# Expert tiles that eleven routed batches fill run in the drain of the batch pipeline, and rows are added to the output by DMA

## The chip, the cores and the metric

One NeuronCore of a Trainium2 chip. The metric is the device time of one launch in microseconds (us). The core's engines run side by side and each takes its own instructions in order: PE (TensorE, matmuls), DVE (VectorE), ACT (ScalarE), POOL (GpSimd), SP (SyncE, which here only issues DMAs). They meet at semaphores alone. POOLq, ACTq and SPq in rows are the sequencers of those engines.

## What is computed

A transformer block with adaptive layer norm (16 batches of 256 tokens, width 128, 16 heads of width 8), followed by a mixture of 8 experts with the 2 best per token:

```python
mod = (_silu(c) @ wmod).reshape(B, 6, 1, -1)          # sa ca ga sb cb gb; |ga|, |gb| at least 0.25
h = _layernorm(x) * (1 + ca) + sa
x = x + ga * attention(h)                             # causal, rotary
h = _layernorm(x) * (1 + cb) + sb
xn = rmsnorm(h) * ln_w
vals, idx = top_k(xn @ Wg + bg, 2); topk_w = softmax(vals)
ffn = sum over the 2 chosen experts e of
      topk_w[e] * ((silu(xn @ W1a[e] + b1a[e]) * (xn @ W1b[e] + b1b[e])) @ W2[e] + b2[e])   # hidden width 512
x = x + gb * ffn
```

## The kernel before

**The pipeline over batches** (`pipeline`, L300) runs iterations i = -3 to 19. In iteration i each engine works on several batches at once, each in another stage: normalise (i+3), projections (i+2), scores by query for the maxima (i+1), probabilities and values (i, i-1), residual and second norm ("routing", batch i-2: `gate_out` L817, the residual add on POOL L492, statistics, `rstd` L506, `xhat` L767, `h_s` L512, `h_m` L514, `square` L637, `rms` L524), logits, top 2 and rank within the expert ("placing", batch i-3: `route` L833, `place` L858), and the sending of rows ("sending", batch i-4: `place_rows` L865 on DVE, `send_rows` L475 on POOL). An iteration is twelve steps k = 0 to 11 on PE, ACT and DVE; the order of the work within a step is written out by hand. On POOL the order of an iteration is the order of the lines L484 to L527. From i = 16 no new batch enters; iterations 16 to 19 are the drain: routing ends with i = 17, placing with 18, sending with 19.

**Routing by DMA.** Each expert has a region of DRAM rows (`expert_rows`), filled from its start. `send_rows` scatters 128 token rows in one indirect DMA of POOL, four times per batch (2 token blocks by 2 chosen experts); a row holds 128 words (the normed token as fp16 high and low part), a token number and the weight, 528 B in all. `filled` on DVE holds how many rows each expert has.

**The table.** After the pipeline DVE computes in 18 dependent steps (L970 to L1012) which expert and which first row each of NT = 39 tiles of 256 rows has. SP and ACT write a dummy tile behind the last row of each expert (`pad_experts`, L335), and SP waits for these and for all sends before it loads the first tile.

**The tile loop**, tile j on each engine:
- SP `load` (L433): waits until tile j-4 has been turned and named, reads the first row from the table and loads 256 rows to `g_in` (4 buffers).
- PE: `hidden` (L1304) computes for four blocks f of the hidden width 6 matmuls of 256 columns each, three for W1a and three for W1b (high x high, high x low, low x high); after f = 1 `turn_rows` (L1290) transposes the rows of tile j+1; then `project_out` (L1325) of tile j-1 with 24 matmuls into one of two banks.
- ACT (L703): silu of each block (L710), `xt` of the next tile (L684), the high part `hh` (L690), and `weigh` (L692) of tile j-2: two scalings by the token's weight into `y_sb` (L699).
- DVE (L1020): h32 = (b + bias) * silu (L1029), the low part `hl` (L1016), and the output bias (L1044) of tile j-2.
- POOL `scatter` (L556): copies number and weight of tile j+2, waits for the weighing of tile j, and writes its rows with two indirect DMAs (L563) to `expert_outs`, one row per token and chosen expert. No scatter waits for the one before it; a buffer `y_sb` is free again after four tiles.

**The finish** (SP L451, POOL L572, DVE L1057, ACT L731): for each batch SP loads its rows of `expert_outs` back, POOL adds the two experts' rows, DVE multiplies by gb (L1060) and adds the residual (L1064), ACT's queue stores the result.

Of the kernel before, what the change touches and what calls it, by code (L numbers as in the profile page):

```python
# [33 lines left out]
P = 128  # L34
# [4 lines left out]
HG = 4  # L39
# [3 lines left out]
NT = (B * S * K + E * (TS - 1)) // TS  # L43
REGION = B * S + TS
ROWS = E * REGION + TS
ROWW = D + 4
W_IDX, W_WGT = D, D + 1
NOUT = B * S * K
# [19 lines left out]
C_COS, C_SIN, C_E, C_BASE, C_TOK, C_POW, C_J = 0, 8, 24, 32, 40, 44, 48  # L68
# [34 lines left out]
def build(nc, x_in, wq, wk, wv, wo, ln_w, wg, bg, w1a, b1a, w1b, b1b, w2, b2, c_in, wmod, const32,  # L103
          const16, constb, dummy_in, out):
    ctx = ExitStack()
    with ctx:
# [11 lines left out]
        outs = nc.dram_tensor("expert_outs", [NOUT, D], F32).ap()  # L118
# [83 lines left out]
        tab = sb("tab", [P, 8, E])  # L202
        tab_i = sb("tab_i", [P, 2, E], I32)
        cmp_j = sb("cmp_j", [P, NT + 1, E])
# [11 lines left out]
        early = probs[:].rearrange("p j t -> p (j t)")  # L216
        silu_a = early[:, 0:FB * TS].rearrange("p (f t) -> p f t", t=TS)
        h32 = early[:, FB * TS:2 * FB * TS].rearrange("p (f t) -> p f t", t=TS)
        y_sb = early[:, 2 * FB * TS:2 * FB * TS + 4 * NS * D].rearrange("p (r s d) -> p r s d", s=NS, d=D)


        gb_sb = v_aug[:, 0:2].rearrange("p r c j g w -> p (r c j g w)").rearrange("p (b d) -> p b d", d=D)
        free = we_lo[:].rearrange("p n f -> p (n f)").bitcast(F32)

        def last(start, blocks):
            return free[:, start * NS * D:(start + blocks) * NS * D]

        y_in = last(0, 8).rearrange("p (r s k d) -> p r s k d", s=NS, k=K, d=D)
        ysum = last(8, 4).rearrange("p (r s d) -> p r s d", s=NS, d=D)
        ygate = last(12, 4).rearrange("p (r s d) -> p r s d", s=NS, d=D)  # L230
        res = last(16, 4).rearrange("p (r s d) -> p r s d", s=NS, d=D)

# [3 lines left out]
        chain_a16, chain_b16 = chain_a[:].bitcast(F16), chain_b[:].bitcast(F16)  # L236
# [7 lines left out]
        mod_out, gb_in = sem("mod_out"), sem("gb_in")  # L244
# [38 lines left out]
        table = sem("table")  # L283
# [6 lines left out]
        pe_y, vec_y, act_y = sem("pe_y"), sem("vec_y"), sem("act_y")  # L290
        y_sent = [sem(f"y_sent{r}") for r in range(4)]
        y_back = [sem(f"y_back{r}") for r in range(4)]
        pool_sum, vec_gate, vec_res = sem("pool_sum"), sem("vec_gate"), sem("vec_res")
        out_done = [sem(f"out_done{r}") for r in range(4)]

        TABLE_STEPS = 18
# [15 lines left out]
        def experts_of(eng):  # L312
# [10 lines left out]
            def read_next(j):  # L323
                m, r, _ = j
                if r == 3:
# [4 lines left out]
            for n in range(2):  # L330
                eng.reg_mov(before[n], 0)
            eng.load(regs, tile_e[0:1, 0:4])
            return known, read_next

        def pad_experts(eng, first):  # L335

            ends = [eng.alloc_register(f"end{n}") for n in range(4)]
            eng.load(ends, tab_i[0:1, 0, first:first + 4])
            for end in ends:
                v = eng.snap(end, min_val=0, max_val=ROWS - TS)  # L340
                eng.dma_start(rows[bass.ds(v, TS), :].rearrange("(s p) w -> p s w", p=P), dummy_sb[:]).then_inc(padded, 16)
# [14 lines left out]
        x_view = x_in.rearrange("b (s p) d -> p (b s) d", p=P)  # L356
        w1a_v = w1a.rearrange("e d (h f) -> e h d f", h=NS)
# [7 lines left out]
        def _(sp):  # L365
# [19 lines left out]
            def iteration(i, sending, placing, routing, closing, s2, s1, s0, norm):  # L385
# [22 lines left out]
                if s1:  # L408
                    place_max(i + 1, 1)

# [12 lines left out]
            sp.wait_ge(probs_used, B * 2 * HG)  # L423
            sp.dma_start(gb_sb, mod_rows[:, 3 * D:].unsqueeze(0).broadcast_to([P, B, D])).then_inc(gb_in, 16)
            sp.wait_ge(table, 1)
            pad_experts(sp, 0)
# [4 lines left out]
            sp.wait_ge(table, TABLE_STEPS)  # L431

            def load(j):  # L433
                r = j[1]

                if due(times(plus(j, -4), 1, 1)):
                    sp.wait_ge(pe_x, times(plus(j, -4), 1, 1))
                    sp.nop(nofuse=True)
                    sp.wait_ge(named.sem, named.after(plus(j, -4), "weight"))
                    sp.nop(nofuse=True)  # L440
                v = sp.value_load(tile_row[0:1, bass.ds(times(j, 1), 1)], min_val=0, max_val=ROWS - TS)
                sp.dma_start(g_in[:, r, :, :], rows[bass.ds(v, TS), :].rearrange("(s p) w -> p s w", p=P)).then_inc(g_arrived[r], 16)

            in_fours(sp, 0, NT, load)

# [3 lines left out]
            back = outs.rearrange("(b s p k) d -> b p s k d", s=NS, p=P, k=K)  # L449

            def finish(n):  # L451
                m, r, _ = n
                if due(times(plus(n, -4), 1, 1)):
                    sp.wait_ge(pool_sum, times(plus(n, -4), 1, 1))
                sp.dma_start(y_in[:, r], back[times(n, 1)]).then_inc(y_back[r], 16)

            in_fours(sp, 0, B, finish)
            for r in range(4):
                sp.wait_ge(out_done[r], 16 * (B // 4))
# [942 lines left out]
```

## Time and profile before

| | us |
|---|---|
| median of 3 runs | 564.38 |
| lowest, highest | 563.98, 567.52 |
| the profiled execution: its own time | 564.96 |
| its span, first to last instruction | 563.1 |

The span is 1.9 us shorter than the profiled execution's own time. Busy shares of the span: PE 80%, DVE 78%, ACT 66%, POOL 58%. An average over the whole says little here, since the program has four stages with different limits. Times in rows are from the span's start.

### The profile page before, as it was taken

What the parts mean: (1) busy time and instruction counts of PE and PEld (TensorE: products, weight loads), DVE (VectorE), ACT (ScalarE), POOL (GpSimd) and SP (SyncE); (2) the same over time, 40 slices, a digit from 0 to 9 for tenths busy, and PEclk for the clock granted to TensorE, in tenths of its full rate; (3) what the DMA queues carried; (4) which work ended last, traced back from release to release, by engine and by line L of the source; (5) the groups of instructions that cost most, each with busy time, mean ns of one, the idle gap of its engine ahead of it and who ended that gap; (6) DMA issues with size and microseconds to landing.
All of it is one profiled execution on the core that took longest, in us unless ns stands there. A gap on an engine that the chain in (4) does not pass through costs nothing.

```text
span 563.1 us, 20014 instructions
## 1 busy us (share of the span) xinstructions
PE 451.6 (80%) x6425; PEld 327.0 (58%) x6426; DVE 438.5 (78%) x1378; ACT 369.4 (66%) x916; POOL 325.0 (58%) x469
## 2 busy tenths in 40 slices
PE   4689999998988988889889313999999999999300
PEld 2445556665555655555555212988888888888300
DVE  4478888999999999999984661777777777777366
ACT  2347777877768777776864221988889888898300
POOL 3433355677777777877766772145455554545553
PEclk9999999999899999998995555999999999999855
DMA  7311111122102222022111323122222112121086
GB/s 216 122 30 46 33 34 39 55 69 63 61 16 69 69 64 59 18 67 70 36 42 40 99 77 102 31 59 66 53 57 59 48 53 57 50 57 36 15 266 181
DMA packets 46920, 37.74 MB, mean 67 GB/s; under 512 B 9234, under 2 KB 41573, under 8 KB 46848
## 3 DMA queue, kind: packets, MB, share of 16 engines
q1 hardware_dynamic: 36288, 25.05, 16.3%
q0 software_dynamic: 4544, 8.54, 4.7%
q10 hardware_dynamic: 6016, 3.21, 1.9%
q8 instruction: 43, 0.70, 0.5%
q14 instruction: 29, 0.24, 0.1%
HBM read 24.77 MB, written 12.78 MB: 67 GB/s over the span
## 4 chain that ended last, share of the span: by engine, by line
PE 35%; DVE 34%; issue 10%; ACT 8%; DMA 4%; SPq 4%; POOL 2%; DVEq 1%; ACTq 1%; POOLq 0%
DVE nmax L799 8%; PE bank L1315 4%; PE bank L1316 4%; PE bank L1317 4%; PE bank L1127 3%; DVE xhat L767 3%; PE bank L1336 3%; DVE probs L1029 3%; ACT qk_t L670 2%; PE bank L1169 2%; PE bank L1337 2%; PE bank L1134 2%; DVE hl L1016 2%; PE bank L1147 2%; PE bank L1338 2%
## 5 line engine op out<-in xcount | busy, mean ns | idle before, releaser
L563 POOL DMA_INDIRECT expert_outs<-probs,number_of x78 | 78.6, 1007 | 95.1 <-ACT probs L699 80.3
L799 DVE TENSOR_REDUCE nmax<-bank 128x2 f16<-128x384 f32 (+1 forms) x192 | 114.8, 600 | 20.6 <-PE bank L1134 18.5
L611 ACT ACTIVATE probs<-bank 128x512 f32<-128x512 f32 (+1 forms) x192 | 100.6, 524 | 45.6 <-PE bank L1159 44.6
L1029 DVE SCALAR_TENSOR_TENSOR probs<-bank,b_sb,probs 128x256 f32<-128x256 f32 x156 | 71.7, 479 | 53.0 <-ACT probs L710 52.3
L1127 PE MATMUL bank<-qk_t 24*64 24x64 f16 (+3 forms) x1024 | 74.5, 246 | 28.5 <-DVE nmax L799 19.4
L1315 PE MATMUL bank<-xt,we_hi 128*128 128x256 f16 x312 | 86.2, 276 | 2.8 <-DVE probs L1029 1.2
L1316 PE MATMUL bank<-xt,we_hi 128*128 128x256 f16 x312 | 86.0, 276 | 0.0
L1317 PE MATMUL bank<-xt,we_lo 128*128 128x256 f16 x312 | 85.9, 275 | 0.0
L480 POOL DMA_INDIRECT expert_rows<-send,pos_i x64 | 64.7, 1010 | 26.0 <-DVE tok L884 14.3
L690 ACT ACTIVATE hh<-probs 128x256 f16<-128x256 f32 x156 | 64.2, 411 | 20.3 <-DVE probs L1029 18.2
L1147 PE MATMUL bank<-qk_t 32*64 32x256 f16 (+3 forms) x1024 | 72.5, 240 | 1.7 <-DMA qk_t<-nmax_t 1.6
L1127 PEld LDWEIGHTS bank<-qk_t 24*64 24x64 f16 x1024 | 33.0, 107 | 68.5 <-DVE nmax L799 35.3
L710 ACT ACTIVATE probs<-bank,b_sb 128x256 f32<-128x256 f32 x156 | 68.3, 462 | 4.0 <-PE bank L1317 3.0
L1336 PE MATMUL bank<-we_hi,hh 128*128 x312 | 57.1, 222 | 4.7 <-DVE hl L1016 4.3
L1016 DVE TENSOR_TENSOR hl<-probs,hh 128x256 f16<-128x256 f32 x156 | 58.5, 416 | 0.0
L1338 PE MATMUL bank<-we_hi,hl 128*128 x312 | 55.3, 221 | 0.0
L1337 PE MATMUL bank<-we_lo,hh 128*128 x312 | 55.3, 221 | 0.0
L1169 PE MATMUL bank<-probs,v_aug 128*32 128x256 f32 (+3 forms) x1024 | 52.0, 324 | 0.0
L1134 PE MATMUL bank<-cb,c 128*128 128x128 bf16 (+1 forms) x192 | 48.9, 255 | 0.0
L1159 PE MATMUL bank<-cb,c 128*128 128x128 bf16 (+1 forms) x192 | 46.7, 243 | 0.0
L1147 PEld LDWEIGHTS bank<-qk_t 32*64 32x64 f16 x1024 | 35.9, 106 | 4.7 <-DMA qk_t<-nmax_t 2.2
L1336 PEld LDWEIGHTS bank<-we_hi,hh 128*128 128x128 f16 x312 | 30.8, 99 | 12.5 <-issue 11.6
(157 smaller groups left out, 1087.3 us busy)
## 6 DMA issues: line engine op xcount, KB each, us to landing
g_in<-expert_rows SPq DMA_DIRECT2D x39, 132.0 KB
qk_t<-nmax_t SPq DMA_DIRECT2D x256, 0.5 KB
mod_b<-mod_rows SPq DMA_DIRECT2D x16, 256.0 KB
we_lo<-expert_outs SPq DMA_DIRECT2D x16, 256.0 KB, 3.8
wstage<-in_L_ffn_W1a_dram SPq DMA_DIRECT2D x16, 128.0 KB
wstage<-in_L_ffn_W1b_dram SPq DMA_DIRECT2D x16, 128.0 KB
wstage<-in_L_ffn_W_dram SPq DMA_DIRECT2D x16, 128.0 KB
out_dram<-we_lo ACTq DMA_DIRECT2D x16, 128.0 KB, 3.4
```

Source lines behind the costliest of these rows:

```text
L563: pool.indirect_dma_start(out=outs, out_offset=bass.IndirectOffsetOnAxis(ap=number_of[:, r, s:s + 1], axis=0), in_=y_sb[:, r, s, :], in_of ...
L611: nc.scalar.activation(probs[:, k // 3, first:end], col_bank[k % 2][:, 0:end - first], ACT.Exp, scale=SM_SCALE).then_inc(probs_ready, 1)
L710: nc.scalar.activation(silu_a[:, f], banks[f][:, 0:TS], ACT.Silu, bias=b1_sb[:, 0, bass.ds(e * FB + f, 1)]).then_inc(act_silu, 1)
L799: nc.vector.tensor_reduce(nmax[:, pair, js[0]:js[-1] + 1, 3 * DK + c], scores, AX.X, ALU.max, negate=True).then_inc(max_ready, 1)
L1016: nc.vector.tensor_tensor(hl[:, j[1] % 2, f], h32[:, f], hh[:, j[1] % 2, f], ALU.subtract).then_inc(vec_hl, 1)
L1029: nc.vector.scalar_tensor_tensor(out=h32[:, f], in0=banks[f][:, TS:2 * TS], scalar=b1_sb[:, 1, bass.ds(e * FB + f, 1)], in1=silu_a[:, f], ...
L1127: mm(row_bank[u % 2][ROW * n:ROW * n + ROW, seg * m:seg * m + seg], qk_t[rows_g, b % 3, j, ROW * c:ROW * c + ROW], qk_t[rows_g, b % 3, HG ...
L1147: mm(col_bank[k % 2][ROW * n:ROW * n + ROW, at:at + S - ROW * c], qk_t[group, b % 3, HG + j0 + jn, ROW * c:ROW * c + ROW], qk_t[group, b % ...
L1315: mm(o, we_hi[:, n, at], x_hi, start=(n == 0), stop=False, skip_group_check=True)
L1316: mm(o, we_hi[:, n, at], x_lo, start=False, stop=False, skip_group_check=True)
L1317: t = mm(o, we_lo[:, n, at], x_hi, start=False, stop=True, skip_group_check=True)
L1336: mm(o, hh[:, par, f, tok_s], we_hi[:, 2, at], start=(s == 0 and f == 0), stop=False, skip_group_check=True)
```

## The change

- **Two tables.** When 11 batches have been placed, DVE copies the counts (`count_early`), and in iteration 15 it computes a first table (`first_tiles`) of the EARLY = 15 tiles that these rows are sure to fill. The second table (`last_tiles`), for tiles 15 to 38, is computed in iteration 19, spread over its steps.
- **Tiles in the drain.** In each step k of iterations 16 to 19 PE, ACT and DVE first do one block f of one tile (`tile_step`), so 3 tiles per iteration and tiles 0 to 11 in the drain. SP loads tiles 0 to 3 at the end of iteration 15 and three per drain iteration. POOL does tile 0's scatter in iteration 16, three in each of 17, 18 and 19 (the one of tile `drained - 2` ahead of everything else in the iteration, two later). Tiles 12 to 14 follow, then 15 to 38 in the loop.
- **The output is added up in DRAM.** x after attention is stored to `out` per batch (SP, iteration i for batch i-2). Each scatter adds its rows to `out` by an indirect DMA with an add (`compute_op=ALU.add`). A token's two rows may lie in neighbouring tiles, so each scatter waits until the scatter before it has landed (`y_sent`). `expert_outs` and the finish are gone.
- **The gate rides in the row.** gb of the batch is put into the row to send (`gates`, one DMA of SP per batch), so a row is 260 words (1040 B) instead of 132, and a tile's load 260 KB instead of 132 KB. `weigh` is moved from ACT to DVE: y times weight times gate, two instructions. Therefore `load(j)` also waits for the weighing of tile j-4.
- One PSUM bank instead of two for the turned rows (`chain_b`) and for y (`o_bank`), since the drain uses the others. In the drain the exponential of the routing is a power on POOL, so that ACT keeps its table for silu. All eight pads are issued by SP.

```diff
+EARLY_B = 11
+EARLY = -(-(EARLY_B * S * K - E * (TS - 1)) // TS)
-ROWW = D + 4
+ROWW = 2 * D + 4
@@ sync, end of iteration(i)
+                if routing:
+                    sp.wait_ge(pool3a.sem, pool3a.after(i - 2, "resid"))
+                    sp.dma_start(out_view[:, NS * (i - 2):NS * (i - 1), :], x_sb[:, NS * (i - 2):NS * (i - 1), :]).then_inc(x_out[i - 2 >= EARLY_B], 16)
+                if placing:
+                    gates(i - 3)
+                if i == B - 1:
+                    sp.wait_ge(early_table.sem, len(early_table.names))
...
+                    for n in range(4):
+                        load(tile_number(n))
+                if i >= B:
+                    n = 3 * (i - B) + 3
+                    for n in range(max(n, 4), n + 3):
+                        load(tile_number(n))
@@ load(j)
+                    sp.wait_ge(vec_w, times(plus(j, -4), NS, NS))
+                    sp.nop(nofuse=True)
@@ sync, after the pipeline
+            sp.wait_ge(last_table.sem, last_table.after(0, "ends"))
+            pad_experts()
...
+            sp.wait_ge(last_table.sem, len(last_table.names))
+            in_fours(sp, EARLY, NT, load)
-            in_fours(sp, 0, B, finish)
@@ gpsimd, iteration(i)
+                drained = 3 * (i - B)
+                if i == B:
+                    pool.wait_ge(x_out[0], 16 * EARLY_B)
+                    name_rows(tile_number(0))
+                    name_rows(tile_number(1))
+                if i > B:
+                    scatter(tile_number(drained - 2))
...
+                if i > B and not i == B + 3:
+                    scatter(tile_number(drained - 1))
...
+                if placing and i >= B:
+                    nc.gpsimd.tensor_tensor(egap[:], c32[:, C_EXP:C_EXP + NS], gap[:], ALU.pow).then_inc(gap_exp, 1)
+                if B <= i < B + 3:
+                    scatter(tile_number(drained))
...
+                if i == B + 3:
+                    scatter(tile_number(drained - 1))
+                    scatter(tile_number(drained))
@@ scatter(j)
-                pool.wait_ge(act_y, times(j, NS, NS))
+                pool.wait_ge(vec_w, times(j, NS, NS))
+                before = plus(j, -1)
+                if due(times(before, 1, 1)):
+                    pool.wait_ge(y_sent[before[1]], times((before[0], 0, 1), 32, 32))
                 pool.nop(nofuse=True)
                 for s in range(NS):
-                    pool.indirect_dma_start(out=outs, ..., bounds_check=NOUT - 1, oob_is_err=False).then_inc(y_sent[r], 16)
+                    pool.indirect_dma_start(out=out_rows, ..., bounds_check=NOUT - 1, oob_is_err=False, compute_op=ALU.add).then_inc(y_sent[r], 16)
@@ scalar
-                    if f == 2 and finished:
-                        weigh(plus(j, -2))
@@ vector
+                if i == B - 2:
+                    count_early()
...
                 for k in range(NK):
+                    if i >= B:
+                        tile_step(*tile_of(i, k))
...
+                    if i == B - 1 and k == 3:
+                        first_tiles()
+                    if i == B + 3:
+                        last_tiles(k)
@@ vector, tile_step(j, f)
+                if f == 0 and finished:
+                    bias_out(plus(j, -2), before_last)
+                vec.wait_ge(act_silu, times(j, FB, f + 1))
...
+                if f == 0 and finished:
+                    weigh(plus(j, -2))
+            def weigh(j):
+                r = j[1]
+                vec.wait_ge(vec_y, times(j, 1, 1))
+                vec.wait_ge(named.sem, named.after(j, "weight"))
+                if due(times((j[0], 0, 1), 32)):
+                    vec.wait_ge(y_sent[r], times((j[0], 0, 1), 32))
+                vec.nop(nofuse=True)
+                for s in range(NS):
+                    nc.vector.scalar_tensor_tensor(out=y_sb[:, r, s], in0=yb[:, r % 2, s], scalar=weight_of[:, r, s:s + 1],
+                                                   in1=g_in[:, r, s, W_GATE:], op0=ALU.mult, op1=ALU.mult).then_inc(vec_w, 1)
@@ tensor
                 for k in range(NK):
+                    if i >= B:
...
+                        tile_step(*tile_of(i, k))
```

## Rows read from the trace of the kernel before

**Rows 1.** The page: the span in 40 equal slices, in tenths
```profile
PE   4689999998988988889889313999999999999300
...
PEclk9999999999899999998995555999999999999855
```
**Rows 2.** Busy time by stage; columns as named in its second line
```profile
core 0: us, PE busy (x) PEld busy (x) DVE busy (x) ACT busy (x) POOL busy (x), PEclk, DMA share, GB/s
...
304.80:318.00 13.20, 9.04 (x58) 5.68 (x58) 7.68 (x39) 3.28 (x12) 8.38 (x12) 0.50 0.31 90
318.00:329.40 11.40, 2.94 (x14) 2.33 (x14) 6.02 (x34) 2.59 (x9) 8.36 (x10) 0.50 0.11 38
329.40:343.60 14.20, 0.28 (x5) 0.19 (x4) 7.53 (x39) 2.42 (x4) 8.39 (x9) 0.50 0.40 119
343.60:361.50 17.90, 14.79 (x143) 12.66 (x144) 8.32 (x22) 11.16 (x29) 0.96 (x7) 0.77 0.21 54
361.50:532.60 171.10, 160.97 (x1887) 139.87 (x1885) 126.22 (x330) 145.03 (x401) 88.82 (x149) 0.99 0.19 51
532.60:563.10 30.50, 0.00 (x0) 0.00 (x0) 19.07 (x32) 0.00 (x0) 13.85 (x17) 0.50 0.68 206
```
**Rows 3.** The scatter line L563: ns min/median/max, first and last start
```profile
L563 POOL DMA_INDIRECT expert_outs<-probs,number_of x78: 971/979/1130, 361.5 to 532.6; - x78
...
DMA to landing us min/median/max: 2.1/2.3/3.8
```
**Rows 4.** The chain that ended last, 529 to 542: start us, us, what
```profile
529.83 0.70 ACT probs L699 x2
...
531.34 0.97 POOL expert_outs L563
532.31 0.30 issue
532.62 2.11 DMA expert_outs<-probs,number_of
```
**Rows 5.** POOL in order of time, 515 to 563 (last scatter, finish)
```profile
531.34 0.97 POOL L563 DMA_INDIRECT expert_outs<-probs,number_of  x1 [0.86 <-ACT probs L699]
532.62 0.97 POOL L563 DMA_INDIRECT expert_outs<-probs,number_of  x1 [0.30 <-issue]
```
**Rows 6.** Transfers and table on the chain, 280 to 348
```profile
294.56 1.54 DMA qk_t<-nmax_t
...
343.67 2.22 DMA g_in<-expert_rows
```
**Rows 7.** POOL in order of time, 298 to 346 (one drain iteration)
```profile
306.80 0.73 POOL L492 TENSOR_TENSOR x_sb<-x_sb,gated 128x256 f32<-128x256 f32 x1 [1.97 <-DVE gated L821]
308.44 0.99 POOL L480 DMA_INDIRECT expert_rows<-send,pos_i  x1 [0.92 <-DVE tok L884]
309.46 0.68 POOL L499 TENSOR_TENSOR send<-xn,send 128x256 f16<-128x256 f32 x1
...
314.69 0.72 POOL L524 TENSOR_TENSOR rms<-ms,c 128x2 f32<-128x2 f32 x1 [0.42 <-DVE rank L860]
```
**Rows 8.** POOL in order of time, 440 to 450 (naming of a tile)
```profile
446.42 0.21 POOL L553 COPY number_of<-g_in 128x2 int32<-128x2 int32 x1
446.54 0.20 POOL L554 COPY weight_of<-g_in 128x2 f32<-128x2 f32 x1
```
**Rows 9.** Groups of DVE: the tile loop's, and the nearest to weighing
```profile
L1029 DVE SCALAR_TENSOR_TENSOR probs<-bank,b_sb,probs 128x256 f32<-128x256 f32 x145 | 66.5, 479 | 38.8 <-ACT probs L710 38.1 <-issue 0.5
L1016 DVE TENSOR_TENSOR hl<-probs,hh 128x256 f16<-128x256 f32 x147 | 55.1, 416 | 0.0
...
L831 DVE SCALAR_TENSOR_TENSOR xn<-h_m,rms,lnw_sb 128x128 f32<-128x128 f32 x8 | 2.4, 342 | 1.1 <-POOL rms L524 1.1
```
**Rows 10.** PE alone in stretches of 2 us: us, PE busy (x), granted clock, DMA
```profile
348.00:350.00 2.00, 2.00 (x12) 0.50 0.32 78
350.00:352.00 2.00, 2.00 (x14) 0.52 0.21 58
352.00:354.00 2.00, 2.00 (x22) 1.00 0.27 68
```
**Rows 11.** DVE in order of time, 280 to 346 (first and last table step)
```profile
333.51 0.17 DVE L972 CAST tab_i<-filled 128x8 int32<-128x8 f32 x1
...
338.39 0.18 DVE L1011 CAST tile_e<-tj 128x40 int32<-128x40 f32 x1
```

More of the change, by code:

```diff
@@ L117, in build @@
         rows = nc.dram_tensor("expert_rows", [ROWS, ROWW], F32).ap()
-        outs = nc.dram_tensor("expert_outs", [NOUT, D], F32).ap()
         c32 = sb("c32", [P, NC32])
@@ L282, in build @@
         sent = [sem("sent0"), sem("sent1")]
-        table = sem("table")
+        early_table = steps("early_table", "clear count count_i tiles_i tiles weight sum cmp e part offset row0 row row_i expert expert_i left done")
+        last_table = steps("last_table", "ends count count_i tiles_i tiles left sum next net weight cmp e part offset row0 row row_i expert expert_i")
         padded = sem("padded")
@@ L328, in read_next, with read_first, is_tile, tile_of @@
                     eng.load(regs, tile_e[0:1, bass.ds(4 * (m + 1), 4)])
[L330 to L341, printed above, removed]
+            def read_first():
+                eng.wait_ge(early_table.sem, len(early_table.names))
+                for n in range(2):
+                    eng.reg_mov(before[n], 0)
+                eng.load(regs, tile_e[0:1, 0:4])
+            return known, read_next, read_first
+        def is_tile(j, n):
+            return isinstance(j[0], int) and j == tile_number(n)
+        def tile_of(i, k):
+            step = NK * (i - B) + k
+            return tile_number(step // FB), step % FB
         def in_fours(eng, first, end, body):
@@ L690, in high @@
                 nc.scalar.activation(hh[:, j[1] % 2, f], h32[:, f], ACT.Copy).then_inc(act_hh, 1)
-            def weigh(j):
-                r = j[1]
-                if due(times((j[0], 0, 1), 32)):
-                    act.wait_ge(y_sent[r], times((j[0], 0, 1), 32))
-                act.wait_ge(vec_y, times(j, 1, 1))
-                act.wait_ge(named.sem, named.after(j, "weight"))
-                for s in range(NS):
-                    nc.scalar.activation(y_sb[:, r, s], yb[:, r % 2, s], ACT.Copy, scale=weight_of[:, r, s:s + 1]).then_inc(act_y, 1)
@@ L739, in _, with tile @@
+            def tile(j, more=True):
+                for f in range(FB):
+                    tile_step(j, f, more)
+            pipeline(iteration)
+            for n in range(3 * FB, EARLY):
+                tile(tile_number(n))
+            in_fours(act, EARLY, NT - 1, tile)
+            tile(tile_number(NT - 1), more=False)
         @block.vector
@@ L1010, in _, with count_early @@
-            vec.wait_ge(table, 17)
-            nc.vector.tensor_copy(tile_e[:], tj[:, 0]).then_inc(table, 1)
-            vec.wait_ge(table, TABLE_STEPS)
+            base, iota = c32[:, C_BASE:C_BASE + E], c32[:, C_J:C_J + NT + 1]
+            each, padded_each = slice(1, E + 1), slice(0, E + 1)
+            count, tiles, zero, ends, done, left, weight, net = (tab[:, n] for n in range(8))
+            def count_early():
+                nc.vector.memset(tab[:], 0.0).then_inc(early_table.sem, 1)
+                vec.wait_ge(early_table.sem, early_table.after(0, "clear"))
+                vec.wait_ge(vec_place.sem, vec_place.after(EARLY_B - 1, "filled"))
+                nc.vector.tensor_tensor(count[:, each], filled[:], base, ALU.subtract).then_inc(early_table.sem, 1)
@@ L1325, in project_out, with tile @@
+                t.then_inc(pe_ab, 1)
+                if f == 1 and more:
+                    turn_rows(plus(j, 1))
+                if f == FB - 1:
+                    if due(times(j, 1)):
+                        project_out(plus(j, -1), last)
+                    read_next_experts(j)
+            def tile(j, more=True):
+                e = known_experts(j)[0]
+                for f in range(FB):
+                    tile_step(j, f, more)
+                return e
             def project_out(j, e):
@@ L1339, in project_out @@
                 t.then_inc(pe_y, 1)
-            def tile_and_last(j, more=True):
-                e, last = hidden(j, more)
-                project_out(plus(j, -1), last)
-                return e
-            turn_rows(tile_number(0))
-            hidden(tile_number(0))
-            in_fours(pe, 1, NT - 1, tile_and_last)
-            project_out(tile_number(NT - 1), tile_and_last(tile_number(NT - 1), False))
+            pipeline(iteration)
+            for n in range(3 * FB, EARLY):
+                tile(tile_number(n))
+            in_fours(pe, EARLY, NT - 1, tile)
+            project_out(tile_number(NT - 1), tile(tile_number(NT - 1), False))
 def constants():
```

405 lines of the change are left out of this document (218 added, 187 removed).

## The prediction

> **What bounds the kernel now.** I read the page's slices first [rows 1]: PE is dense in two blocks, with a hole between them in which the granted clock is at its lower level, and empty at the end. The busy time by stage puts numbers on it [rows 2]. From 304.8 (the last probabilities of batch 15 are just done) to 343.6 (the first load of a tile) lies the drain with the table and the pads: 38.8 us in which PE is busy for 9.04 + 2.94 + 0.28 = 12.3 us, and that at clock 0.50, so it is some 6.1 us of work at full clock. From 343.6 to 532.6 runs the tile loop with PE busy nearly throughout. From 532.6 to 563.1 PE has nothing: the last scatter lands and the finish reads, adds and stores.
>
> The tile loop's rate is read from its scatters [rows 3]: 78 issues start from 361.5 to 532.6, the second of a tile 1.28 after the first [rows 5], so 38 tiles take 171.1 - 1.28 = 169.8 us, 4.47 us each.
>
> The new thing is the wait of each scatter for the landing of the one before, so the length of one scatter matters. The chain at the end shows it unhidden [rows 4]: the weighing ends at 530.53, POOL's first indirect DMA starts at 531.34 (0.81 to wake), takes 0.97, 0.30 of issue, and the second transfer's 2.11 begin at 532.62. The list of POOL [rows 5] has the second issue start at that same 532.62: the landing counts from the start of the issue, not from its end. So a plain scatter needs 0.81 + 0.97 + 0.30 + 2.11 = 4.19 us from release to landing; with the median landing of 2.3 [rows 3] it is 4.38. That is 0.1 under the tile's 4.47, before anything is paid for the add.
>
> **The change part by part.**
>
> *The add.* No row of before shows an indirect DMA that adds. It has to read the old row from DRAM as well. From below: nothing, if that read runs beside the read of the new one. A gain is excluded, since it does all that the plain write does. From above: a whole second landing, 2.3. Nearest are two transfers [rows 6]: SBUF to SBUF lands in 1.54, DRAM to SBUF in 2.22; a DRAM read in the way costs 0.7 (sizes differ, so this is rough). I take 0.7: a scatter in a chain of scatters takes P = 4.38 + 0.7 = 5.1 us, bounds 4.4 and 6.7. The issue itself (0.97) I leave as it is; if it grew by half, P would grow by 1.0, which is inside these bounds.
>
> *The loop when P is above the tile's time.* POOL then sets the rate; PE, ACT and DVE wait through the four `y_sb` buffers (`weigh(j)` waits for scatter j-4). The naming of the next tile (0.21 + 0.20 [rows 8]) lies in the landing, which outlasts the issue by 2.3 - 0.98 = 1.3.
>
> *The weighing moves to DVE.* Nearest is the 128x128 product at 0.342 us [rows 9]: two make 0.7. DVE's tile was four of 0.479, four of 0.416 and one output bias of about 0.42: 4.0 in sum of durations (neighbours overlap in the rows), of which 126.2/38.3 = 3.3 busy [rows 2]. With 0.7 it stays at 4.0 of 4.47: it fits, and ACT loses as much. Cost 0, at worst 0.2 a tile, hidden while P is 5.1; without this cover it is 27 x 0.2 = 5 us.
>
> *Larger load, later released.* `load(j)` now starts only after `weigh(j-4)`, in DVE's tile j-2, and PE turns its rows in tile j-1, about 4.5 us later. The load needs the register read and issue, about 0.9, and 2.22 for half the bytes [rows 6]; I put 2.7 on 260 KB: 3.6. It fits with 0.9 to spare. Behind the waiting SP stand only further loads. Were a load to land in 4.3 as the worst 256 KB ones may, PE would stall some tenths per tile; P covers that too.
>
> *One bank for y and one for the turned rows.* `project_out(j)` waits for the bias add of j-1, which DVE does while PE spends 24 of 48 matmuls on the hidden blocks of j+1; nothing is paid. The same for the turned rows: their copy ends a half tile before.
>
> *The drain.* Iterations 16 to 19 now hold 12 tiles. Three sizes of it can be had. PE alone: 12 x 4.47 + 6.1 = 60 us. Nothing overlapped: 38.8 + 53.6 = 92 us. And POOL, which is in order and has the most to do. Its own work per full iteration is five elementwise operations of 0.7 and four sends of 0.99 with 0.3 each [rows 7], 8.4 busy [rows 2], 9.6 with gaps. A scatter adds 2 x 0.98 + 2 x 0.3 + 0.3 for the names, 2.85, and about 0.45 where it has to be woken: 3.3; the landing of the one before is covered by the work between, except for the last two. Iteration 16 took 13.2 for its waits; with one scatter, a second naming and the power (0.8) it is 17.4. Iteration 17: 9.6 + 0.8 + 3 x 3.3 = 20.3. Iteration 18, without the residual and norm, has four sends (5.1), 0.7, 0.8 and three scatters: 16.5. Iteration 19: four sends, one scatter, and two in a chain at P: 5.1 + 3.3 + 10.2 = 18.6. Sum 73 us. I take POOL's sum, since PE's 60 lies under it and the steps lock the engines together. At 304.8 PE is at the lower clock; it rose about 5 us after PE became dense at 347 [rows 10], so iteration 16 loses a few us on PE, which POOL's 17.4 covers.
>
> *Tables and pads.* 18 steps took from 333.5 to 338.6, 5.1 us [rows 11]. The first table is some 16 of them, narrower, about 3.5 us, in iteration 15, where DVE waits in places anyway; I count 1 us. The second lies in iteration 19 beside POOL's 18.6. Pads and the wait for the last sends then have tiles 12 to 14 (15 us) as cover; without these they cost the 3 to 4 us that they did.
>
> *Main part.* SP gets two DMAs more per iteration (gate, x), each some 0.5 us of its queue, behind the second `place_max`; what waits for SP next is a maximum of the next iteration, half of it later. Rows sent are twice as long. Counted as 0, at worst 0.5 x 16 = 8.
>
> *Removed.* The finish: from 532.62 + 2.11 = 534.7 to 563.1, 28.4 us.
>
> **The sum.** 304.8 + 1 (first table) + 73 (drain, scatters 0 to 9 landed) + 29 x 5.1 (scatters 10 to 38, the last landing included) = 304.8 + 1 + 73 + 147.9 = 526.7 span. The profiled execution's time is 1.9 above its span and the median 0.6 below that time: 528 us.
>
> **The rivals.**
>
> *A. The tile sets the rate.* If the add costs under 0.1 to 0.2, POOL follows PE again. For it: the plain scatter is 0.1 shorter than the tile. Against: an add without any cost. After the drain 27 tiles x 4.5 and the tail of the last one (before: last matmuls near 527.4 to landing at 534.7, with the last hidden part 8.3): 304.8 + 1 + 73 + 121.5 + 8.3 + 1.3 = 510 us.
>
> *B. The drain does not overlap.* POOL waits inside a scatter for `weigh`, DVE waits at `rstd` or `rms` for POOL, PE for DVE, so that latencies add. For it: in-order queues, and each of the old iterations is itself such a chain. Against: the scatters are placed behind the step that frees them. With 92: 304.8 + 1 + 92 + 147.9 + 1.3 = 547 us.
>
> *C. The other side: the add doubles the landing.* Place: POOL's wait for `y_sent` in each scatter. Price: 2.3 more, P = 6.7, and 304.8 + 1 + 73 + 29 x 6.7 + 1.3 = 574 us. It decides from P = (564.4 - 380.1)/29 = 6.4 on. For it: all 29 scatters of the last part stand in one chain, each 0.1 us is 2.9 us. Against: the rows are 512 B, eight per DMA engine and issue, so latency and not volume makes the landing. The Trainium skill speaks for this rival: "Collectives: The Full Stack" (The bandwidth ceiling) says that a reduction in the DMA engines needs two source reads on one ring and measured 1.93 times the time of a copy. By it the landing would be 4.4, P 6.5 and the kernel 568 us; no row of before shows an adding DMA.
>
> **How the numbers follow.** Forecast 0.55, A 0.23, B 0.12, C 0.10. A measurement tells about 1% from no change: faster is under 558.7, slower over 570. The forecast, A and nearly all of B are faster; C is slower, and a P near 6.2 falls in between: 0.83, 0.08, 0.09. The range reaches from under A, 507, to P = 6.0 or B with a somewhat dearer add, 556.
>
> **What would show it.** Right: after the drain POOL's line of the adding DMA has starts 5.1 apart per tile, and its idle time is ended by the landing of `out`, not by DVE; PE waits about 0.7 a tile for DVE; the landing is 3.0. The drain is 73 us with the clock at its upper level after the first few us. The span ends with a landing. The forecast is wrong if the period differs from 5.1 by over 0.3 (9 us), if POOL waits for the weighing (A), if the drain is over 85 (B), or if the landing is over 4.3 (C).

## The result and the profile after

The changed kernel takes 703.37 us, median of four runs (702.48 to 708.62), beside 564.92 (563.98 to 567.52) for the one before: ratio 1.246, 95% interval 1.239 to 1.254. Forecast were 528 us and a range of 507 to 556. The profiled execution has a span of 700.4 us, 173.7 over the forecast's sum of 526.7.

First the page after, the slices of [rows 1] (each is 17.5 us now).

```profile
span 700.4 us, 20061 instructions
...
PE   4889994955955846856755827766767977877820
...
PEclk9999997868778879768878657989987999999965
```

PE loses its density from slice 7 on, some 105 us in, in the middle of the old pipeline, in which I had changed nothing by my own count. The hole of before at slices 23 to 25 is gone, but nearly every slice behind the seventh is thinner, and the last two (2 and 0) are close to empty again, though there is no finish any more.

Where the time came from is read by stage. The borders are now the end of POOL's 48th send of rows (304.8 in [rows 2]), the landing of scatter 9, the end of PE's work but for its last 1.2 us, and the end. The landing is set at 519.9, the median 3.3 us behind the start of the issue; this one in fact landed at 522.9, so 3 us of the chain's part below belong to the drain's. The first line is of the kernel before, for the same work as the line below it.

```profile
core 0: us, PE busy (x) PEld busy (x) DVE busy (x) ACT busy (x) POOL busy (x), PEclk, DMA share, GB/s
60.00:304.80 244.80, 219.60 (x3822) 140.29 (x3818) 225.34 (x786) 178.07 (x416) 174.12 (x233) 0.97 0.18 51
...
60.00:415.70 355.70, 239.91 (x3852) 149.93 (x3850) 236.95 (x801) 178.46 (x417) 174.32 (x234) 0.80 0.22 58
415.70:519.90 104.20, 74.09 (x786) 63.51 (x787) 71.91 (x262) 57.59 (x146) 65.34 (x79) 0.86 0.43 99
519.90:673.00 153.10, 117.14 (x1311) 97.81 (x1310) 101.49 (x280) 91.44 (x225) 86.70 (x100) 0.95 0.40 67
673.00:700.40 27.40, 1.22 (x12) 0.95 (x9) 1.65 (x5) 0.00 (x0) 12.66 (x11) 0.50 0.12 9
```

| part | forecast | measured | off by |
|---|---|---|---|
| start to the end of the pipeline | 305.8 | 415.7 | +109.9 |
| drain, to the landing of scatter 9 | 73 | 104.2 | +31.2 |
| scatters 10 to 38 | 147.9 | 180.5 | +32.6 |
| finish | 0 | 0 | 0 |

ACT and POOL are busy as long as they were before: POOL has its 174 us of work, now in 355.7 us in place of 244.8. So this is waiting. The groups of waits name it (us in total, times, longest):

```profile
POOL expert_rows L498 <- DMA send<-mod_rows: 116.2, 12, 12.1
PEld bank L1211 <- DVE nmax L811: 115.1, 42, 9.9
...
DVE xhat L779 <- POOL rstd L531: 90.8, 12, 10.2
ACT qk_tok L700 <- POOL turned L566: 82.4, 12, 9.3
```

The first of these is the source and the others are its echo: POOL waits twelve times, some 10 us each, for the DMA that puts the gate into the rows to be sent; DVE and ACT wait for POOL, PE for DVE. One such iteration on the queue of SP and then on POOL (start, us, instruction, and in brackets the idle time before it):

```profile
342.21 4.38 SPq L459 DMA_DIRECT2D qk_t<-nmax_t  x8
346.65 0.40 SPq L411 DMA_DIRECT2D out_dram<-x_sb  x1
347.09 0.54 SPq L450 DMA_DIRECT2D send<-mod_rows  x1
```

```profile
330.58 0.98 POOL L498 DMA_INDIRECT expert_rows<-send,pos_i  x1 [9.37 <-DMA send<-mod_rows]
...
345.67 0.73 POOL L517 TENSOR_TENSOR x_sb<-x_sb,gated 128x256 f32<-128x256 f32 x1
...
356.56 0.99 POOL L498 DMA_INDIRECT expert_rows<-send,pos_i  x1 [10.16 <-DMA send<-mod_rows]
```

This is a ring. POOL is let into its first send at 330.58. Behind that send stand the power, the turning and the keys of the next batches; from these PE makes scores and DVE maxima, whose DMAs SP issues until 346.59. Only then comes the gate's DMA, at 347.09. It takes 8.5 us to land (its line's median), and POOL is let into the next first send at 356.56. That is 16.5 + 9.5 = 26.0 us, and an iteration is 26.9 long between two residual additions where it was 17.4 (typical distances).

The scatter line, for [rows 3] and [rows 5]:

```profile
L599 POOL DMA_INDIRECT out_dram<-qk_tok,number_of x78: 1538/1549/1958, 442.9 to 694.6; - x78
...
DMA to landing us min/median/max: 2.7/3.3/6.3
```

```profile
563.45 1.55 POOL L599 DMA_INDIRECT out_dram<-qk_tok,number_of  x1 [2.29 <-DMA out_dram<-qk_tok,number_of]
565.30 1.54 POOL L599 DMA_INDIRECT out_dram<-qk_tok,number_of  x1 [0.30 <-issue]
...
569.22 1.55 POOL L599 DMA_INDIRECT out_dram<-qk_tok,number_of  x1 [2.06 <-DMA out_dram<-qk_tok,number_of]
```

The period (from one tile's first issue to the next tile's) is 5.77 here. Issue went from 0.98 to 1.55, the landing from 2.3 to 3.3. By the forecast's own formula P = 0.81 + 1.55 + 0.30 + 3.3 = 5.96; the mean over tiles 15 to 38 is 5.88, where the forecast had 5.1 and the kernel before 4.40. Most of these waits stand in the trace under the name issue (79.5 us in 69 pieces, only 10.7 under the landing), as the profile saw no releaser. The times tell it: from tile 15 on a scatter starts 0.81 us after the landing of the one before in the median, wherever the trace has that landing, and its own weighing has then been over for 11 us or more. From 673 on PE has a last 1.2 us of work, and POOL goes on through its chain to the end, 27.4 us later.

Right behind the drain the chain is slower than that. SP writes the eight pads there, 260 KB each, and the DMA engines are busy all the time (share 1.00). The landings of the next scatters stretch (median 5.2 us from 508 to 530), and PE waits for a tile's load. The pads, the stretch of time, POOL's scatter 10 and PE:

```profile
L445 SPq DMA_DIRECT2D expert_rows<-dummy_sb x8: 372/397/925, 514.2 to 519.4; - x8
...
514.00:523.00 9.00, 5.89 (x68) 4.95 (x65) 7.11 (x21) 5.30 (x13) 3.47 (x4) 1.00 1.00 273
...
523.67 1.55 POOL L599 DMA_INDIRECT out_dram<-qk_tok,number_of  x1 [5.17 <-issue]
...
528.53 0.61 PE L1390 MATMUL bank<-c,g_in 128*128 128x128 f16 x4 [7.33 <-DMA g_in<-expert_rows]
```

### The profile page after: what moved, and what is told of

The parts are those of the page before. It is cut to its first block and busy times, and to the rows that moved or that the text cites. A ratio compares the mean times of both kernels' runs of the same rounds, so it can differ in the third digit from the quotient of the medians.

```text
span 700.4 us, 20061 instructions
## 1 busy us (share of the span) xinstructions
PE 476.9 (68%) x6425; PEld 338.2 (48%) x6426; DVE 449.3 (64%) x1443; ACT 353.6 (50%) x835; POOL 361.6 (52%) x456
## 3 DMA queue, kind: packets, MB, share of 16 engines
q1 hardware_dynamic: 43760, 33.06, 18.5%
## 5 line engine op out<-in xcount | busy, mean ns | idle before, releaser
L599 POOL DMA_INDIRECT out_dram<-qk_tok,number_of x78 | 123.4, 1582 | 91.5 <-issue 79.5
L1105 DVE SCALAR_TENSOR_TENSOR qk_tok<-bank,b_sb,silu_a 128x256 f32<-128x256 f32 x156 | 73.4, 480 | 48.7 <-ACT silu_a L731 46.5
L779 DVE TENSOR_SCALAR xhat<-x_sb,mv,rstd 128x128 f32<-128x128 f32 x64 | 35.7, 598 | 91.7 <-POOL rstd L531 90.8
L721 ACT ACTIVATE hh<-qk_tok 128x256 f16<-128x256 f32 x156 | 64.5, 413 | 38.9 <-DVE qk_tok L1105 36.6
L731 ACT ACTIVATE silu_a<-bank,b_sb 128x256 f32<-128x256 f32 x156 | 71.4, 468 | 21.3 <-PE bank L1408 20.5
L1253 PE MATMUL bank<-probs,v_aug 128*32 128x256 f32 (+3 forms) x1024 | 60.5, 365 | 0.0
L1092 DVE TENSOR_TENSOR hl<-qk_tok,hh 128x256 f16<-128x256 f32 x156 | 60.1, 427 | 0.0
L1390 PE MATMUL bank<-c,g_in 128*128 128x128 f16 x156 | 16.5, 232 | 57.7 <-DMA g_in<-expert_rows 57.6
L700 ACT ACTIVATE qk_tok<-turned 128x256 f16<-128x256 f32 x32 | 13.2, 411 | 82.6 <-POOL turned L566 82.4
L1218 PE MATMUL bank<-cb,c 128*128 128x128 bf16 (+1 forms) x192 | 50.3, 262 | 0.0
```

The lines of the kernel that those rows point to most:

```text
L599: pool.indirect_dma_start(out=out_rows, out_offset=bass.IndirectOffsetOnAxis(ap=number_of[:, r, s:s + 1], axis=0), in_=y_sb[:, r, s, :], i ...
L721: nc.scalar.activation(hh[:, j[1] % 2, f], h32[:, f], ACT.Copy).then_inc(act_hh, 1)
L731: nc.scalar.activation(silu_a[:, f], banks[f][:, 0:TS], ACT.Silu, bias=b1_sb[:, 0, bass.ds(e * FB + f, 1)]).then_inc(act_silu, 1)
L1105: nc.vector.scalar_tensor_tensor(out=h32[:, f], in0=banks[f][:, TS:2 * TS], scalar=b1_sb[:, 1, bass.ds(e * FB + f, 1)], in1=silu_a[:, f], ...
```

## The experiments

Each is the changed kernel with one edit unless said otherwise; before means a kernel before run on the same chip beside it.

**e1, the gate's place in SP's queue.**

```diff
+                if placing:
+                    gates(i - 3)
                 if s1:
                     place_max(i + 1, 0)
...
-                if placing:
-                    gates(i - 3)
```

> The changed kernel with SP's gate DMA moved ahead of the two groups of max transfers in its iteration; its waits and bytes are the same. Theory G (place in the queue): the changed kernel's batch pipeline is 111 us longer (POOL's last send of iteration 15 ends at 415.7 instead of 304.8), because POOL waits for a gate that SP issues only behind the last maxima and that lands 8.5 us later. Then POOL's 116 us of waiting for the gate go to under 10, the last send of iteration 15 ends at 305 to 320, and the time falls from 703 to 590 to 615. Rival T (traffic: rows twice as long, 16 more DMAs of 256 KB, the stores of x): the pipeline stays over 390 and the time over 680, wherever the gate DMA stands.

Measured: 587.53 us, 1.040 of before (1.026 to 1.055). The same windows:

```profile
60.00:305.80 245.80, 221.98 (x3853) 142.02 (x3846) 225.88 (x801) 178.63 (x417) 174.00 (x233) 0.96 0.35 86
305.80:406.30 100.50, 75.19 (x791) 62.40 (x790) 71.97 (x264) 58.16 (x148) 65.78 (x79) 0.90 0.42 95
406.30:584.10 177.80, 115.14 (x1315) 95.88 (x1312) 101.96 (x283) 90.89 (x224) 99.81 (x110) 0.91 0.35 59
```

The pipeline ends at 305.8, as forecast, with every DMA still issued and the same landing of 8.4: POOL's wait for the gate is gone from the list. So 116 us of the change's time are the place of one DMA in an in-order queue, 110 of them in the pipeline. The time is 2.5 us under the 590 to 615 expected. What is left, 584.1 against 526.7, is drain (+27.5) and chain (+29.9).

**e2, no gate at all.** `gates(i - 3)` and POOL's wait for it are out.

> The changed kernel without the gate DMAs and POOL's wait for them, so the expert part of the output is left out (it is multiplied by zero); every other instruction runs. Theory G: the same gain as with the gate issued first, 590 to 610, and the difference between the two, up to 10 us, is what the gate's 256 KB cost as traffic. Rival T: if the doubled rows and the stores are what slows the pipeline, it stays over 390 at POOL's last send of iteration 15 and the time over 680.

Measured: 581.46 us, 1.030 (1.016 to 1.043). Against e1 that is 6 us, with overlapping intervals, and 8.5 us under the 590 to 610 expected. The pipeline ends at 308.4, no earlier than in e1: in its new place the gate's DMA costs the pipeline nothing. The drain is the shorter part, 92.0 for 100.5 us.

**e11, old place, quicker DMA.** The gate's DMA stays where the change put it, but reads 512 different rows (of `x`) in place of 512 times one row, so the gates are other numbers. **e7** is the same on top of e1.

```diff
-mod_rows[b:b + 1, 3 * D:].unsqueeze(1).broadcast_to([P, K * NS, D])
+x_in.rearrange("(c b2) t d -> c (b2 t) d", b2=2)[b // 2].rearrange("(p n) d -> p n d", n=K * NS)
```

> The changed kernel with the gate DMA where it was, but reading 512 different rows (landing 3.3 instead of 8.4 us; other numbers are multiplied in). It parts the 111 us of the pipeline into place and landing. Theory: each of the 12 waiting iterations gets 5.1 us back, 61 in all: pipeline to 350 to 360, time 635 to 650. Rival (the wait is set by the place alone, behind the last maxima, or the landing alone): over 690, or under 600.

> The kernel with the gate issued first, its DMA reading 512 different DRAM rows of 512 B instead of one row 512 times (other numbers than the gate's are multiplied in). Theory H (the one row read over and over is what makes the landing 8.4 us): it falls to 3 to 4.5 us. Rival D (512 pieces of 512 B into a strided tile cost this anyway): it stays over 7. The time stays within 8 us of 587 by both, since nothing waits for this DMA there.

Measured: e11 626.87 us, 1.113 (1.105 to 1.121), 76 less than the changed kernel; e7 one run of 578.07. The gate's DMA in the changed kernel, in e7 and what waits for it in e11:

```profile
DMA to landing us min/median/max: 8.2/8.5/10.1
```

```profile
DMA to landing us min/median/max: 3.2/3.3/4.6
```

```profile
L450 SPq DMA_DIRECT2D send<-in_L_attn_x_dram x16: 545/594/1531, 108.4 to 406.7; - x16
...
  POOL expert_rows L498: 55.3, 12
```

The same bytes in as many pieces (43760 packets on that queue in both) to the same places land in 3.3 in place of 8.4: reading one DRAM row 512 times is what was slow. In e7 a partition's four rows are neighbours in DRAM; whether that plays a part was not run. And the ring passes it on one for one: 26.9 less 5.2 gives 21.7 per iteration, and e11 has 21.2 in the mean (19.2 to 22.6). Its pipeline ends at 352.0, within the 350 to 360 expected; in all it beat the expectation of 635 to 650, since the drain got some 11 us shorter too. Speed of the DMA alone does not cure the order, though: 12 waits of 4.6 remain. In e7 nothing waits for this DMA, and yet it is 9.5 us under e1, where within 8 was expected: one run, but its drain shows where, as e5 does next.

**e5, the gate fetched once and copied on the chip.** One 64 KB DMA per batch, then a copy by ACT into the rows.

```diff
-dma_start(mod_b[:, i % 2, :], mod_rows[i:i + 1, :].broadcast_to([P, 4 * D]))
+dma_start(mod_b[:, i % 2, :], mod_rows[i:i + 1, 0:3 * D].broadcast_to([P, 3 * D]))
+dma_start(gate_b[:, i % 4, :], mod_rows[i:i + 1, 3 * D:].broadcast_to([P, D]))
...
+activation(send[..., W_GATE:], gate_b[:, bs % 4, :].unsqueeze(1).broadcast_to([P, K * NS, D]), ACT.Copy)
```

> The changed kernel with the gate brought to SBUF once per batch (64 KB, 128 rows of 512 B, beside mod_b) and copied into the rows to send by one ACT instruction, instead of a DMA of 512 rows of 512 B. Theory G: the gate was dear only by its place and landing, so this is within 8 us of the kernel with the gate issued first (587): 580 to 592, and POOL waits for nothing of the gate. Rival: the copy of about 0.6 us on ACT delays the sends and costs 16 x 0.6 = 10 us or more: over 595.

Measured: 576.35 us, 1.024 (1.011 to 1.037), 11 under e1 and 4 under the 580 expected at least, though the intervals of the two overlap. The stages show where. Scatter period 5.88 in both; the drain is 92.0 in place of 100.5. In e1 scatters 2 and 5 (from 0) start 11.85 and 11.23 after the ones before them, here 8.02 and 6.43. PE's wait for loads of tiles is 44.6 us in e1 and 37.6 here. The slow read is what does it: e7 differs from e1 in nothing else and has 8.06 and 8.35 there, and a drain of 96.1. What exactly it holds up was not looked into.

**e3, chain without the add, and e4, add without the chain.** In e3 the scatter overwrites. In e4 every (token, expert) has its own row in `outs` and scatters don't wait for each other.

```diff
-bounds_check=NOUT - 1, oob_is_err=False, compute_op=ALU.add)
+bounds_check=NOUT - 1, oob_is_err=False)
```

```diff
-                before = plus(j, -1)
-                if due(times(before, 1, 1)):
-                    pool.wait_ge(y_sent[before[1]], times((before[0], 0, 1), 32, 32))
```

> The changed kernel with the scatter's add taken away (a plain write, so residual and first expert's row are lost from the output); each scatter still waits for the landing of the one before. Theory A (the add itself is dear): issue back from 1.55 to 0.98, landing from 3.3 to 2.3, a scatter from 5.9 to 4.4 apart; with 29 scatters behind the drain 703 falls by 40 to 50 to about 658. Rival W (the waiting is dear, not the add): scatters stay over 5.3 apart and the time falls by under 20.

> The changed kernel whose scatters add into rows of their own (one row per token and chosen expert in a separate tensor, so the two are not summed and the output lacks the expert part), and therefore need no wait for the scatter before. Theory A with the chain: the wait for the landing is gone, a scatter costs POOL 2 x 1.55 + 2 x 0.3 + 0.3 = 4.0 and a wake, 4.5 to 4.8 apart, and the 27 us tail in which PE has nothing shrinks to under 12; time 650 to 665. Rival (POOL's issue is the bound, not the landing): over 5.3 apart, time over 680.

Measured: e3 658.60 us, 1.166 (1.145 to 1.187), scatter period 4.81 (4.4 was expected); e4 659.49, 1.168 (1.149 to 1.186), period 4.71. Each is 44 to 45 us under the changed kernel. The add and the wait are not two prices that sum: take either away and the chain no longer sets the period alone. From tile 15 on 23 of 24 scatters of e4 start about 0.8 us after their own weighing, and in e3 16 of 24 start within 1.4 us of it. In the changed kernel none does. The line of e3 has the plain price back:

```profile
L599 POOL DMA_INDIRECT out_dram<-qk_tok,number_of x78: 967/978/1516, 439.5 to 646.3; - x78
...
DMA to landing us min/median/max: 2.1/2.8/6.0
```

**e12, the add alone, in the kernel before.** `compute_op=ALU.add` on its unchained scatters; 16 DMAs of SP set the rows to zero during the pipeline.

> The kernel before with the add in its scatters (onto rows that 16 further DMAs of SP have set to zero in the pipeline), no scatter waiting for another. Theory (the add alone is hidden; only in a chain is it paid): POOL's tile is 2 x 1.55 + 2 x 0.3 + 0.3 = 4.0 us, under the tile's 4.47, so the loop keeps its 4.47 and only the last landing and issues come late, 2 to 3 us; with the zeroing 565 to 572. Rival (POOL with a wake of 0.8 is over 4.47 per tile): 4.8 per tile, 578 or more.

Measured: 566.07 us, median of ten, 1.0031 (0.9991 to 1.0071). The scatter line and POOL's last issues:

```profile
L571 POOL DMA_INDIRECT expert_outs<-probs,number_of x78: 1543/1552/1845, 360.4 to 532.9; - x78
```

```profile
525.54 1.54 POOL L571 DMA_INDIRECT expert_outs<-probs,number_of  x1 [0.30 <-issue]
527.39 1.55 POOL L571 DMA_INDIRECT expert_outs<-probs,number_of  x1 [0.30 <-issue]
529.24 1.54 POOL L571 DMA_INDIRECT expert_outs<-probs,number_of  x1 [0.30 <-issue]
```

POOL pays 78 x 0.57 = 45 us more for its issues, and the kernel takes the same time: two issues are 3.7 us of a tile that lasts 4.43. An adding scatter is free off the path. In a chain it is 0.57 of issue and 1.0 of landing per tile by the formula; the period fell by 1.1 without it (5.88 to 4.81 in e3), since the weighing then comes about as late as the landing.

**e8, e1 with plain scatters, and e9, e10: the load split.** PE in e1 still waits 44.6 us for tile loads, and a load waits for `vec_w` on account of the gate in it. In e9 (on e1) and e10 (on e8) the x part is loaded without that wait, and the gate part by a DMA of its own:

```diff
-                    sp.wait_ge(vec_w, times(plus(j, -4), NS, NS))
...
-dma_start(g_in[:, r, :, :], rows[bass.ds(v, TS), :]...)
+dma_start(g_in[:, r, :, 0:W_GATE], rows[bass.ds(v, TS), 0:W_GATE]...)
+                if due(times(j, 1)):
+                    load_gate(plus(j, -1))
```

> The kernel with the gate issued first and the scatter's add replaced by a plain write, each still waiting for the one before (residual and first expert's row are lost). Theory A: the same 45 us as in the changed kernel, 587 to 537 to 548; scatter 9 lands 80 to 92 us after the pipeline instead of 100, then 29 scatters of 4.7 to 4.9. Rival (once the gate is out of the way another limit holds the loop): over 560.

> The kernel with the gate issued first and each tile's load in two DMAs: the 132 words with token, number and weight without the wait for the weighing of tile j-4, and the gate's 128 words with that wait, one tile later in SP's order. Theory C (the chain of adding scatters, 5.9 to 6.1 apart, is the bound and PE's 50 us of waiting for loads are only its echo): the loop stays at 6.0 per tile, only the drain may lose up to 10: 575 to 588. Rival L (the late load is a bound of its own): 560 or less.

> The same two DMAs per load in the kernel with the gate issued first and plain scatters in a chain. Here the scatters (4.4 of release to landing) leave room, and PE waited 68 us for loads against 8 us in the part with the short rows. Theory L (load released by the weighing is the next limit under the add): PE's wait for loads falls under 25 us and the time from 540 to 518 to 532. Rival (the plain chain of 4.4 plus what POOL waits for the weighing is the bound): 536 or more.

Measured: e8 543.69 us (two runs, 539.46 and 547.91; its rows are of the longer one), within its 537 to 548 and 44 under e1, so the add has about the same price with and without the ring; e9 591.21, 1.049 (1.041 to 1.058); e10 538.54, 0.956 (0.949 to 0.962). The expectation's 68 us of waiting for loads in e8 counts PE's 32.5 and the weight load's 35.2 for the same loads. PE's group of the turned rows (busy, mean ns, then idle before it) in e9 and in e10:

```profile
L1401 PE MATMUL bank<-c,g_in 128*128 128x128 f16 x156 | 16.8, 236 | 31.8 <-DMA g_in<-expert_rows 31.8
```

```profile
L1401 PE MATMUL bank<-c,g_in 128*128 128x128 f16 x156 | 15.5, 224 | 9.1 <-DMA g_in<-expert_rows 9.1
```

e9 missed its 575 to 588: PE waits 13 us less for loads, and the period is 5.97, as before the edit (5.88). A late load was the echo of a late POOL. In e10 the waits shrink from the 32.5 of e8, and the period stays too, 4.76 after 4.77; it missed its 518 to 532, and is within 1 us of the quicker run of e8. So the load is not what holds the plain chain at 4.8, either. By the formula a plain chain has P = 0.81 + 0.98 + 0.30 + 2.3 to 2.8 = 4.4 to 4.9, which would do it. e4, with no chain, has 4.71 because POOL waits for the weighing. Why the tile itself takes 0.3 longer there than before (two products more on DVE, longer loads, for which PE waits 6.4 us from 540 on) was not taken apart.

**e6, the early tiles alone.** Two tables and tiles in the drain stay. Rows are short again, scatters plain, without a chain and into own rows, gate and sum in the finish of before; the weighing stays on DVE, as a product with one scalar. This computes the whole output.

```diff
-ROWW = 2 * D + 4
+ROWW = D + 4
...
-scalar_tensor_tensor(out=y_sb[:, r, s], in0=yb[:, r % 2, s], scalar=weight_of[:, r, s:s + 1], in1=g_in[:, r, s, W_GATE:], ...)
+tensor_scalar(y_sb[:, r, s], yb[:, r % 2, s], weight_of[:, r, s:s + 1], None, ALU.mult)
...
-oob_is_err=False, compute_op=ALU.add)
+oob_is_err=False)
```

> One part of the change alone: two tables and tiles in the drain, with the row of 132 words, no gate in it, plain scatters without a chain into expert_outs and the finish of the kernel before. Theory (the tiles in the drain are worth what was forecast, add and gate ate it): pipeline to 306, drain 70 to 85 with 12 tiles in it, 27 tiles of 4.5 and the tail of 8, finish 28: 533 to 550 us, faster than before by 3 to 5%. Rival B (the drain does not overlap with the tiles even without the add, latencies add): drain over 92, time over 555, no gain left.

Measured: 543.52 us, median of five; 0.9665 of before (0.958 to 0.975), within the 533 to 550 expected. It beats both kernels. Its windows, from its quickest run (537.58): drain, tile loop, finish.

```profile
303.20:382.00 78.80, 66.18 (x704) 57.23 (x704) 63.37 (x242) 50.33 (x129) 52.34 (x77) 0.89 0.23 63
382.00:508.70 126.70, 113.85 (x1399) 102.46 (x1396) 104.89 (x303) 96.69 (x242) 67.01 (x112) 1.00 0.23 63
508.70:535.50 26.80, 0.00 (x0) 0.00 (x0) 18.85 (x32) 0.00 (x0) 13.35 (x16) 0.50 0.76 235
```

In [rows 2] the drain was 38.8 us with PE busy for 12.3; here PE is busy for 66.2 of 78.8. The period of tiles 15 to 38 is 4.18, under the 4.40 of before, with the weighing off ACT (the edit nearest to this; it wasn't run alone). The finish it keeps costs 26.8 us.

## Why the prediction was wrong, by its own steps

- *Main part* is the step that failed, with nearly two thirds of the miss (109.9 of 173.7 us). It listed the two new DMAs of SP and asked what waits behind them on SP ("what waits for SP next is a maximum of the next iteration"), priced that at 0, at worst 8 us, and never asked who waits for the DMAs themselves. POOL's first send does (`pool.wait_ge(gate_in...)` in `send_rows`), it stands ahead of everything from which SP's next maxima come, and the DMA comes after these maxima. The two orders close to a ring of 26 us around a pipeline step of 17.4. The wait was in the diff, and the ring could have been summed: nearly a whole step of 17.4 from the first send to the last maxima (16.5 it was), then a landing and a wake, so over 17.4 with any landing. e1 shows the place to be the cause; e11 shows that the length of the DMA goes into it one for one.
- *The same step* gave that DMA no landing at all. It is 8.5 us (3.3 with different source rows), and this excess is 5.2 x 12 = 62 of the 110. No row above showed such a read; the nearest in the trace of before is `v_aug<-mod_rows`, 1024 KB from 16 rows of 512 B, each read 128 times, which landed in 9.3.
- *The add*: the mechanism was right, the size off. I took 0.7, on the landing alone; measured are 1.0 on the landing and 0.57 on the issue, which I had left "as it is". P came out at 5.96 by the formula, inside my bounds of 4.4 and 6.7, and at 5.88 in the mean (5.4 to 6.5) between scatters. My "if it grew by half, P would grow by 1.0" counted both issues of a scatter; my formula has one of them, as the landing counts from the start of the second, so it is 0.5. 29 x 0.86 = 25 of the 32.6 us; most of the rest lies right behind the drain, where scatter 10 starts 8.95 after scatter 9 and the next five are 5.8 to 7.4 apart, beside the pads.
- *The drain*: 73 by POOL's sum. With plain, unchained scatters and short rows it is 78.8 (e6). My sum has two scatters in a chain at 5.1; at 3.3 each and with a last landing of 1.3 it is about 71, so the method falls some 8 us short. With the price of the add, 10 scatters x 2 x 0.57 = 11.4 more, the sum is 84; measured 92.0 with the copied gate (e5), 100.5 with the slow one (e1), 104.2 as changed, and 107.2 to the landing itself. It ended above the 85 at which I had said that it fails. What makes the last 8 us of e5 (chain, longer rows, the store of x) was not taken apart.
- *The weighing on DVE* at 0 was right where the chain covers it: it is done 11 us or more before its scatter. Without this cover the runs differ. In e4 POOL waits for it and the tile has 4.71; in e6, where it is a product with one scalar and the rows are short, the tile got shorter by 0.22. No run has the weighing alone on the other engine.
- *Larger load*: "it fits" was right in effect. It lands in 3.0 (2.7 forecast), and freeing it of its wait gained nothing (e9, e10).
- *One bank, names, tables*: nothing of them shows. The first table was counted as 1 us, and the pipeline of e1 ends 1.0 later than that of before, all of its other additions included; but e6, e7 and e2 end at 303.2, 304.2 and 308.4, so this is luck as much as measure.
- *The pads* were to have tiles 12 to 14 as cover. They do not hide: no tile load is issued from 513.3 to 525.5, PE waits 7.3 us for one, and the landings beside them stretch. In e4, where no chain covers it, scatter 13 starts 14.4 us after scatter 12.
- *Removed*: 28.4 us of finish are gone, as forecast; the tail of POOL, 27.4 us behind PE, took their place. I had that tail in the sum, as part of 29 P.

Of the rivals, A is out: with the add POOL never waits for the weighing in the last part, where each scatter finds its own done long before. B's price of 92 for the drain was nearer than my 73, though in e5 11.4 of the 19 us between 73 and 92 are the add's issue and not latencies that add up. C has the right sign and the wrong reason. The landing of the adding scatter is 3.3 to 2.3, 1.43 times the plain one. The Trainium skill's "Collectives: The Full Stack" (The bandwidth ceiling) has 1.93 for a reduction's two reads, measured at 16 MB. An estimate from it is a landing of 4.4 and a P of 6.5; measured are 3.3 and 5.88, and the measurement decides. Why the ratio is smaller for 128 rows of 512 B, no run shows. Even with the queue mended (e1) the kernel is slower, 584.1 in span, outside my range: a drain 27 us and a chain 30 us dearer than forecast outweigh the 36 us that the forecast had gained (563.1 to 526.7).

## What to carry to other kernels

When a step gets a new DMA, ask two questions of it: who waits behind it on its queue, and who waits for *it*; then go once around from the consumer back to the place in the queue and compare the sum with the loop's step. An issue that needs nothing of this iteration goes ahead of those that do. Before scatters are made to wait for each other, compare wake + issues + landing with the time of a tile: the add was free in the open (e12) and cost 45 us in the chain.

## What was not expected of the hardware

- 128 partitions x 4 pieces of 512 B, all from one DRAM row, land in 8.4 us; the same from 512 different rows in 3.3. The broadcast of a whole 2 KB row to 128 partitions (`mod_b`, 256 KB as well) lands in 3.3, and 1024 KB from 16 rows of 512 B, each read 128 times, in 9.3 (before). So it is not every repeated read that is slow.
- An indirect DMA with an add holds POOL for 1.55 us in place of 0.98 (e12 beside before, nothing else changed on that line), besides its longer landing.
- POOL's two small copies that name a tile are 0.21 and 0.20 in [rows 8]; beside an adding issue (it starts at 559.27 and lasts 1.57) they last 0.76 and 0.75. They lie in the landing, so it costs nothing here.

```profile
559.27 1.57 POOL L599 DMA_INDIRECT out_dram<-qk_tok,number_of  x1 [0.30 <-issue]
560.29 0.76 POOL L586 COPY number_of<-g_in 128x2 int32<-128x2 int32 x1
560.41 0.75 POOL L587 COPY weight_of<-g_in 128x2 f32<-128x2 f32 x1
```
